# Message-passing layer on one core: a gather that waits for VectorE's first vector product, and three steps in other places

## What is computed

```python
r = edge_vec / norm(edge_vec);  sh1 = SQRT3 * r
w = mlp(emb, fc1_w1, fc1_w2)                      # Wss, Wvv, Wsv, Wvs: 128 columns each
vdot1 = einsum('euk,ek->eu', v1, sh1) / SQRT3     # the dot products
s_t = a1 * (einsum('eu,euw->ew', s1, Wss) + einsum('eu,euw->ew', vdot1, Wvv))
v_t = a1 * (einsum('eu,euw->ew', s1, Wsv)[:, :, None] * sh1[:, None, :] + einsum('euk,euw->ewk', v1, Wvs))
w2 = mlp(emb, fc2_w1, fc2_w2)                     # Ass .. Cvs: 64 columns each
vdot2 = einsum('euk,ek->eu', v_t, sh1) / SQRT3
scal, gates = a2 * (s_t x Ass + vdot2 x Avv), a2 * (s_t x Bss + vdot2 x Bvv)
vecs = a2 * ((s_t x Csv) * sh1 + v_t x Cvs)
edge_out = concat([tanh(scal), vecs * tanh(gates)]) * norm
out = layernorm(x + segment_sum(edge_out, edge_dst))
```

## Time and profile before

| | us |
|---|---|
| median of 3 runs (lowest to highest) | 6613.86 (6610.04 to 6614.21) |
| the profiled execution | 6605.81 |
| its span, first to last instruction | 6604.0 |
| busy: PE / DVE / ACT / POOL | 5916.6 / 5987.5 / 4058.7 / 5021.9 |
| share of the span: PE / DVE / ACT / POOL | 90% / 91% / 61% / 76% |
| mean granted clock of TensorE | 0.972 |

### The profile page before, as it was taken

How to read it: one execution, slowest core, us unless ns; L and a number is a source line. 1 busy time by engine, 2 the same in 40 slices (tenths; PEclk the granted TensorE clock), 3 DMA queues, 4 the chain that set the end, 5 groups by cost and what they waited for, 6 DMA issues and landing times.

```text
span 6604.0 us, 217789 instructions
## 1 busy us (share of the span) xinstructions
PE 5916.6 (90%) x67802; PEld 5648.0 (86%) x67802; DVE 5987.5 (91%) x7727; ACT 4058.7 (61%) x12100; POOL 5021.9 (76%) x6871
## 2 busy tenths in 40 slices
PE   2999999999999999999999999999989999999997
PEld 2888888888888888888888888888888888888887
DVE  6999999999999999999999999999999999999998
ACT  3666666666666666666666666666666666666664
POOL 4777777777777777777777777777777777777774
PEclk9999999999999999999999999999999999999998
DMA  4444444444444444444444444444444444444442
GB/s 126 86 89 84 86 87 85 85 87 86 84 86 88 84 87 86 84 86 88 84 86 88 84 86 88 84 88 86 86 89 84 86 88 84 88 86 86 87 85 54
DMA packets 1671528, 569.93 MB, mean 86 GB/s; under 512 B 1535556, under 2 KB 1619493, under 8 KB 1670946
## 3 DMA queue, kind: packets, MB, share of 16 engines
q1 hardware_dynamic: 1568321, 516.43, 35.3%
q0 software_dynamic: 103168, 53.03, 6.0%
HBM read 302.19 MB, written 7.26 MB: 47 GB/s over the span
## 4 chain that ended last, share of the span: by engine, by line
PE 75%; issue 13%; DVE 5%; ACT 3%; another core or an unknown queue 3%; DVEq 1%; ACTq 0%; DMA 0%; POOL 0%; SPq 0%; POOLq 0%
PE p L982 42%; PE pw L977 18%; PE p L1068 4%; PE ph L965 2%; PE ph L954 2%; PE p L1061 2%; PE p L1063 1%; PE p L1029 1%; PE p L1011 1%; DVE prods L1275 1%; ACT hot_t L741 1%; PE p L1012 1%; DVEq L1434 1%; ACT osum L820 0%
## 5 line engine op out<-in xcount | busy, mean ns | idle before, releaser
L982 PE MATMUL p<-identity,prods 128*128 128x128 f32 x29016 | 3642.6, 279 | 7.8 <-issue 6.7
L647 POOL DMA_INDIRECT nodes<-x_rows,idx x3224 | 3114.5, 966 | 603.7 <-issue 515.9
L982 PEld LDWEIGHTS p<-identity,prods 128*128 128x128 f32 x29016 | 3292.0, 146 | 36.5 <-issue 12.3
L977 PE MATMUL pw<-w_stack,hid_t 128*128 128x128 bf16 x22568 | 1702.4, 223 | 116.2 <-issue 52.4
L977 PEld LDWEIGHTS pw<-w_stack,hid_t 128*128 128x128 bf16 x22568 | 1433.6, 100 | 216.7 <-issue 98.2
L1275 DVE TENSOR_TENSOR prods<-pw,M 128x1024 f32<-128x1024 f32 x806 | 977.1, 1212 | 38.5 <-PE pw L977 24.8
L1233 DVE TENSOR_TENSOR prods<-pw,V 128x2048 f32<-128x2048 f32 x403 | 914.4, 2269 | 9.4 <-ACT acc L926 6.3
L1252 DVE TENSOR_TENSOR prods<-pw,S 128x1024 f32<-128x1024 f32 x403 | 491.8, 1220 | 327.6 <-remote 190.7
L838 ACT ACTIVATE off_hot<-node_iota,off_base 128x42 f32<-128x42 f32 x3216 | 752.6, 317 | 13.0
L1285 DVE TENSOR_TENSOR prods<-pw,VT 128x1536 f32<-128x1536 f32 x403 | 705.2, 1750 | 23.9 <-PE pw L977 19.4
L594 POOL TENSOR_TENSOR msg<-th,late 128x128 f32<-128x128 f32 x403 | 164.0, 407 | 728.7 <-ACT th L819 390.8
(11 more groups left out here) (130 smaller groups left out, 8205.5 us busy)
## 6 DMA issues: line engine op xcount, KB each, us to landing
dstb<-in_dst SPq DMA_DIRECT2D x403, 504.0 KB
nodes<-x_rows,idx POOLq DMA_INDIRECT x3224
emb_stack<-emb_parts SPq DMA_DIRECT2D x2418, 20.0 KB
emb<-in_emb_t SPq DMA_DIRECT2D x403, 40.0 KB
hid_t<-hid_parts SPq DMA_TRANSPOSE x806
idx<-in_src SPq DMA_DIRECT2D x403, 4.0 KB
xw<-x SPq DMA_DIRECT2D x403, 7.9 KB
vecs<-in_vec SPq DMA_DIRECT2D x403, 12.0 KB
```

What stands on the lines that cost most here:

```text
L647: nc.gpsimd.indirect_dma_start(nodes[:, p, t, side, :], None, x_rows, bass.IndirectOffsetOnAxis(ap=idx[:, p, side, t:t + 1], axis=0)).then ...
L977: mm = nc.tensor.matmul(pw[:, slot, t, :], hid_t[:, layer, a.par, t, :], w2_stack[:, lo:lo + W], start=True, stop=True)
L982: return nc.tensor.matmul(out, column, identity[:, :], start=first, stop=last, is_transpose=True)
```

## The change

Four things move, all within a turn, and no arithmetic changes. On GpSimd, gather 2 now stands behind a wait for the first vector product of the present group (`pv_done`, which L1233 signals first, and L1237 second), and the second addition of the dot products stands behind gather 3 instead of ahead of gather 1. On ScalarE the features' second piece stands behind the vector sums out, instead of ahead of the hidden layer's second pieces. On VectorE both steps of q stand behind the dot products, where the first stood ahead of them.

```diff
             def along_rest(a):
                 pool.wait_ge(vr_done, a.n(1, 1))
                 nc.gpsimd.tensor_tensor(vr_two[:, :, :], ..., ALU.add).then_inc(vr_two_done, 1)
+
+            def along_last(a):
+                p = a.par
                 pool.wait_ge(vr_two_done, a.n(1, 1))
                 nc.gpsimd.tensor_tensor(S[:, p, :, 2 * C:4 * C], vr_two[:, :, :], vr[:, 2, :, :], ALU.add
                                         ).then_inc(vdot_done, 1)
...
                     if one is not None and i != -1:
                         directions(one)
+                    if two is not None:
+                        pool.wait_ge(pv_done, two.n(2, 1))
+                        pool.sem_inc(gathers_begun, 1)
                     if zero is not None:
                         gathers(zero, 0, (2,))
                     if three_on is not None:
                         emb_less_first(three_on)
                     if zero is not None:
                         gathers(zero, 0, (3,))
+                    if two is not None:
+                        along_last(two)
                     if four is not None:
                         messages_scalar(four, windows, more)
...
+                    if zero is not None:
+                        hidden_second(zero)
+                    if two is not None:
+                        vector_sums_out(two)
                     if three_on is not None:
                         emb_second(three_on)
-                    if zero is not None:
-                        hidden_second(zero)
-                    if two is not None:
-                        vector_sums_out(two)
...
+                    if two is not None:
+                        dot_products(two, ring)
                     if four is not None:
                         q_first(four)
-                    if two is not None:
-                        dot_products(two, ring)
-                    if four is not None:
                         q_second(four)
```

More of the change, by code:

```diff
@@ L905, in body @@
                         rows_laid_out(one, is_general, (1, 0))
-                    if three_on is not None:
-                        emb_second(three_on)
                     if zero is not None:
@@ L911, in body @@
                         vector_sums_out(two)
+                    if three_on is not None:
+                        emb_second(three_on)
                     if two is not None:
@@ L1415, in body @@
                         cross_products(two, ring)
-                    if four is not None:
-                        q_first(four)
                     if two is not None:
@@ L1420, in body @@
                     if four is not None:
+                        q_first(four)
                         q_second(four)
```

## The result

The changed kernel took 6446.75 us (median of 4 runs, 6439.65 to 6460.26) where the kernel before took 6614.03 in the same session: a ratio of 0.9748, 95% interval 0.9727 to 0.9769, or 167 us less. The profiled run took 6460.26 us with a span of 6458.4 and a mean clock of 0.995; before it was 6605.81, 6604.0 and 0.972. The forecast was 6560, so the direction was right and the time lies in the range, but the gain is three times as large as the 54 us of the sum.

A forecast was written before the change was run, and what follows sets the result against it. VectorE, the busiest engine, was taken to bound the kernel, losing 541.4 us to idling. Idling of 467 + 20 = 487 us gave -54: 6552 profiled, 6560 with the runs' median 8 us higher; range 6220 to 6740.

The forecast's parts named there:

- the clear period: Shortest period, nothing holding VectorE up for long: 15.00 us against a mean of 15.99, so 0.99 us idle.
- rival A: Cross products start at 4.46 in every period: 398 us less, some 6215; half the signals slipping through, 6400; chance 0.22.
- Step 1, the start of gather 2: GpSimd's wait for the first vector product, ending at 2.27, puts the gather's start at 2.50 us of the period.
- d: Time from the first vector product's signal to gather 2's start: taken as 0.23 us, bounds 0.16 and 0.64.
- rival B: Gather 2 wakes late, at 2.91 or later; fill 2's signal comes at 6.0 or later: 6678 to 6778 us, chance 0.34.
- Step 1, `osum_t`: ScalarE's copy: transposes' signal comes 0.13 us into gather 2, passes, copy starts at 2.9; TensorE's gap and clock falls go.
- Step 1, fill 2: TensorE's signal for the cross products, held through gathers 2 and 3: 1.16 us idle every period, 467 instead of 327.6.
- Step 2, the second addition: On GpSimd behind gather 3: ends at 5.6, dot products due at 6.7, costs nothing; 0.4 us without that cover.
- Step 3, q: On VectorE behind the dot products: all 102.3 us of idling ahead of L1329 go.
- Step 4, the second piece of the features: On ScalarE behind the vector sums out: nothing or some tenths of a us in some periods.
- Step 5, the rest: VectorE's waits ahead of L1260, L1275 and L1285, nearly all behind clock falls: 20 kept of 111.5 us.
- C: Nothing moves: transposes' signal still held, the wait at L1329 only turns into one for the fill; 6600 to 6625, chance 0.12.

## Why the prediction was right in direction and wrong in size

*What bounds the kernel.* Right on chips with holds: VectorE's idle time is what the period loses, and the hold is real and is caused by gathers (0.927 without two of them). Wrong was the clear period. The earlier trace rows are not of "the shortest kind": L1329 idles 0.47 us in them. The trace of before has 24 of 402 periods below 14.7 us, down to 14.45:

```profile
3336.39 2.27 DVE L1233 TENSOR_TENSOR prods<-pw,V 128x2048 f32<-128x2048 f32 x1
...
3350.84 2.27 DVE L1233 TENSOR_TENSOR prods<-pw,V 128x2048 f32<-128x2048 f32 x1
```

The idle time of the earlier trace rows says so too: 541.4 / 403 = 1.34 us a period, not 0.99. So the prediction's price of rival A, 398 us, was too low for its full form; without gathers 2 and 3 the kernel gains 475. What the traces of one chip could not tell is that other chips have no holds. There the question of the whole forecast, what the change does to 541 us of idling, has no object: with the wait alone (the run at 6063.82 us) VectorE's idle time in the same groups is 0.9 + 7.2 + 9.5 + 0.1 + 0.5 + 28.1 = 46 us.

*Step 1, the start of gather 2.* Wrong in size: d was taken as 0.23 us with bounds 0.16 and 0.64, and it is 0.78, the median in each of nine traces with such a wait, on both kinds of chip. The gap behind L594 in the earlier trace rows is that of a gather behind GpSimd's own work, and the one that a semaphore lets go takes longer to get under way. Nor was it right that nothing stands between wait and gather: the change puts a `sem_inc` of GpSimd there, and what it costs was not run apart. A d of 0.64 or more was the condition of rival B.

*Step 1, `osum_t`.* Right in its result, by another way: the transposes' signal at 2.63 does not slip in 0.13 us into the gather, it comes 0.43 us ahead of it. `osum_t` idles 7.4 us instead of 563.7, TensorE's wait at L1061, 398.6 us "issue" in the waits of before, is 54.4 at L1069, and the clock stays up.

*Step 1, fill 2.* This is the step that failed. I had it held from gather 2 through gather 3 in every period, 403 x 1.16 = 467 us. Measured: 228.7. With d = 0.79 the sum's own way would have given still more, the cross products at 3.06 + 1.60 + 1.52 = 6.18 and 403 x 1.72 = 693 us, so B's side. What is wrong is "that hold meets the next". The semaphore events of the trace after have fill 2's signal some 1.4 us after gather 2's start in 241 of 402 periods, at 4.43 to 4.57 us, about when VectorE is ready (4.46); in 33 it comes some 0.65 and in 127 some 1.43 us after gather 3's start. Without holds it comes at 4.09, so even the 241 are held, but at no cost. So the hold has a gate between the two gathers that is open in three fifths of the periods. The earlier trace rows are of the kind in which it stays closed, and I made a rule of them. Rival A "in part", half of the signals slipping through for 6400 us, was the mechanism that came; it had a chance of 0.22 together with its full form.

*Step 2, the second addition.* I let it cost nothing, and named 0.4 us as its price without cover, for a gather 2 at 2.91. Gather 2 stands at 3.06, and the cover, a late cross product, is missing in three fifths of the periods. It costs: the dot products idle 132.6 us, and 57.6 with the addition back; and without holds 224.4 us, where the whole change loses 260. The condition was in the text, but it was weighed for one start of gather 2 alone.

*Step 3, q.* The wait ahead of q went, as said (102.3 to 8.4, with 13.9 ahead of the second step, which now follows the first directly and waits for it). But the move is not what did it: with the wait alone, with holds and q in its old place, q idles 7.3 us too, and with the moves alone the idle time returns ahead of the dot products.

*Step 4, the second piece of the features.* Nothing can be seen of it: with and without it and q's move the time is the same (0.9708 and 0.9709, on two chips).

*Step 5, the rest.* L1260, L1275 and L1285 were to keep 20 of 111.5 us. The last two keep 6.8; the first, now L1268, has 132.6, by step 2.

*The sum.* 467 + 20 = 487 forecast, 390 measured. The two large errors have opposite signs: a hold that was twice too dear, and a second addition that was not free. The wrong d made the first one smaller: with the right one the rule "held in every period" gives 693 + 20 and a slower kernel. So that the forecast had the right sign, and 6560 within 2% of the measured time, is in part luck.

*Rivals.* C is refuted, as is the array that is late by itself. In the changed kernel TensorE has a new wait, ahead of L1019 (311.8 us "issue" against 21.9 ahead of L1011 before), and the mean clock is 0.995 all the same. The rule of the Trainium skill that I set against the forecast ("TensorE: Matmul & The Clock Gate", section "HAM oscillation — how this bites in real kernels") was taken to keep the low clock through such a wait; the clock did not stay low. But the waits of TensorE in that page's example are several times as long as these, which last 311.8 / 352 = 0.89 us each and 1.6 at most. So it is the prediction's use of the rule that failed, and the trace says nothing against that section.

*Still open.* What decides in which periods the signal passes between gathers 2 and 3. The traces have a strong hint: counted from zero, all 127 periods in which it comes 1.43 us behind gather 3's start are even-numbered ones, also when several clear periods lie between two of them, and so are 142 of 143 in the second trace of the changed kernel, 139 of 139 with the addition back, and 135 of 135 with the wait alone. In the kernel before it is 21 even ones of 38. The buffers and the two PSUM slots change from one period to the next too, but which of that, if any, is the cause was not tried. ScalarE's timing does not explain it: in the held periods its `M` (L811, L806) comes later than in most of the others in the first of these traces (1.8 us against 1.0 to 1.5) and earlier in the last (0.8 to 0.9 against 1.0). Nor is it known what sets chips with holds apart.

## What to carry to other kernels

Time a change of order on more than one chip before it is kept: here the same kernel took 9.5% more on one chip than on another (6614 against 6038 us) and the same edit is worth -2.5% or +4.3%. A wait that pins one queue's start also moves all that stands behind it, so take along what has a due time (the second addition) to the other side of the wait; the wait alone, one edit, was worth at least as much with holds (-2.9%, on another chip than the whole change's -2.5 and -2.1%) and cost 0.36% where there was nothing to win. And a rule such as "held in every period", read from two periods, must be counted over the run before it is multiplied by 403. The same goes for "the shortest kind of period": it is sorted out of all of them, not picked from the timeline.

## What the runs showed of the hardware

- On some chips a signal of TensorE that falls into an indirect gather of GpSimd is delivered late. Of the matmuls that end 1.0 to 1.3 us behind a gather's recorded start 98% signal late (795 of 813 after, 620 of 632 before), and fill 2's signal came about 1.4 us after the start of that gather or 0.65 or 1.43 us after that of the next. On other chips none of these is late (0 of 1173 with the wait alone). The kernel before took 6614, 6610, 6551 and 6551 us in the sessions on the first kind and 6037 to 6043 in those on the second.
- An indirect gather behind a wait for a semaphore (and a `sem_inc`) starts, by its record, 0.78 us after the end of the instruction that signals; one that follows other work of GpSimd starts 0.16 to 0.23 us behind it.
- On a chip with holds a wait of ScalarE for TensorE lowers TensorE's clock at second hand, since TensorE then waits for ScalarE's copy: in the profiled executions the mean granted clock was 0.964 to 0.975 with `osum_t` late (two of the kernel before, one of the moves alone), and 0.994 to 0.995 with `osum_t` in time.
